# Sums of two key tiles added once more by VectorE, in halves, for all pairs but a unit's last

## The chip, the core and the metric

One core of a Trainium2 chip runs the whole program. The metric is the device time of one execution in microseconds. Its engines are TensorE (PE in the profile), VectorE (DVE), ScalarE (ACT), GpSimd (POOL) and SyncE (SP), which issues the DMAs.

## The reference

```python
x = layernorm(x + attention(x, Wq, Wkv, Wo))      # x: 2 x 2048 x 1024, 32 heads of 32, one shared k and v
x = layernorm(x + W x + b + lora(x))              # one of four ranks per row, chosen by a gate
# attention:
scores = einsum('bqhd,bkd->bhqk', q, k) * scale
bias = slopes[:, None, None] * (pos[None, None, :] - pos[None, :, None])
scores = where(causal, scores + bias, -inf)
attn = softmax(scores, axis=-1)
out = einsum('bhqk,bkd->bqhd', attn, v)
```

Only the attention is touched. What matters here is the softmax's denominator: for every query and head, the sum of the exponentials over all keys up to the query.

## The kernel before, in words

The queries of a batch row are cut into four segments of 512 (`QB`, `NSEG`), the 32 heads into eight groups of four (`GH`, `HG`). A **unit** g is one segment and one head group: 2 x 4 x 8 = 64 units, in order, each segment's eight in a row. A unit of segment s (0 to 3) has 4, 8, 12 or 16 **key tiles** of 128 keys (`ktiles`), the last four of them on the diagonal and narrower with each. A **step** k is one key tile; a **slot** is one key tile and one head, so a unit has 16, 32, 48 or 64 slots, and slot number is 4k + h.

For each slot TensorE makes the scores, keys on partitions, 512 queries wide (L895, into one of two or three PSUM banks `ps_s`, `ps_m`), and ScalarE takes the exponential into one of eight SBUF buffers `prob`, each of which holds the four heads of a key tile, 128 x 2048 float32 (L603). A step later TensorE multiplies the exponentials with the values into `ps_o` (plan item PV) and with ones into `ps_sum`, the denominators. Both go through `over_keys` (L828): four matmuls of 32 columns, one per head, which the profile records as eight. Such a set is called a group below.

To save groups on `ps_sum`, GpSimd adds the exponentials of two key tiles, a **pair** (item ADD, L540, in place in the even tile's buffer), once step 2j + 1 has its exponentials (`e_done`) and the even tile's PV is through (`pv_done`). TensorE then needs one group for two tiles (item SP, L912). All pairs are summed but a unit's last (`pairs_summed`: 0, 3, 5 and 7 per unit); the last two tiles, and every tile of the first segment, have groups of their own (SM). In the fourth segment the first two pairs of each unit are added once more by GpSimd (`QUADS = (0, 0, 0, 1)`, item ADDQ, L545), and one group covers four tiles (SQ, L915). GpSimd also splits the next unit's Wq (item WS, L514) and divides the previous unit's output by its denominators (L521). It works through its items in the order of the plan.

Beside this work on unit g, the softmax's shift for the next two units is prepared: item A is a matmul of queries against keys, 128 queries by 512 keys, for its maximum alone (L816, into one of three PSUM banks `ps_a`), which VectorE reduces (L682; L685 with the mask on the diagonal). The matmul for maximum c waits until maximum c - 3 is read (`a_done`, L815). CV reduces the maxima over chunks (L691), CT transposes them (L823, L697). Items Q and QE make the queries of unit g + 2: TensorE's projection into `ps_m` (L782 to L784), then ScalarE (L565) and VectorE (L671) split them. X, KV and VT prepare the next segment's keys and values, R turns and inverts the denominators (L707 to L714), WO loads the output matrix near the end (VectorE's part is L751, a subtraction of two SBUF tensors of 128 x 1024). After the attention follows a part that the change doesn't touch (L920 on).

`plan_unit` (L181) writes out the order of one unit's items, slot by slot; every engine walks the same list and does its part of each item, so it is the instruction order on each queue. The places are the constants in L127 to L143, one value per segment, in slots: `A_END` and `A_FROM` where the maxima of the next unit and of the one after it lie, `CHUNKS_AHEAD` how many of them are made two units ahead, `PV_AT` and `SM_AT` at which head of a step the groups on `ps_o` and `ps_sum` stand, `THIRD` from where the scores may use a third bank. Where items share a slot, the score matmul comes first, then the listed items in the order in which they were put, then PV, SM, SP, SQ.

Of the kernel before, what the change touches and what calls it, by code (L numbers as in the profile page):

```python
# [18 lines left out]
GH = P // DH  # L19
# [55 lines left out]
def pairs_summed(g):  # L75

    return ktiles(g) // 2 - 1 if full_tiles(g) else 0


def quads_summed(g):  # L80

    return QUADS[seg_of(g) % NSEG]


def adds_in(g):
    return pairs_summed(g) + quads_summed(g)


def adds_before(g):
    return sum(adds_in(x) for x in range(g))  # L90


def adds_until(g, k):

    pair = k // 2
    quad = pair // 2
    if quad < quads_summed(g):
        return adds_before(g) + 3 * quad + 1 + pair % 2
    return adds_before(g) + quads_summed(g) + pair + 1


def ring(sg):
# [21 lines left out]

CHUNKS_AHEAD = (7, 14, 18, 19)  # L127
A_END = (8, 17, 31, 41)
A_FROM = (13, 18, 31, 41)
Q_AT = ((0, 0.5), (0, 1), (1, 1.25), (0, 1.75))  # L130
QE_AT = ((3, 1), (7, 2), (9, 3), (12, 4))
CT_AT = (12, 22, 35, 42)
X_AT = ((4, 0.25), (8, 1.75), (19, 1.5), (19, 3.25))
THIRD = (6, 6, 2, 4)
QUADS = (0, 0, 0, 1)
QUAD_AT = 7
WO_AT = ((36, 6), (4, 8))
KV_AT = (10, 23, 33, 41)
VT_AT = (17, 28, 47, 49)
PV_AT = (1, 1, 2, 1)  # L140
SM_AT = (2, 1, 2, 1)
WS_AT = (5, 21, 31, 28)
RECIP_AT = ((0, 2, 3, 4, 11), (0, 2, 3, 5, 14), (0, 2, 5, 7, 18), (0, 2, 4, 5, 20))  # L143


# [35 lines left out]
def plan_unit(g):  # L181
# [6 lines left out]
    def put(slot, what, arg):  # L188
        at.setdefault(min(slots - 1, int(slot)), []).append((what, arg))
# [21 lines left out]
    if g + 2 < UNITS:  # L211
        ahead = a_chunks(g + 2)[:chunks_ahead(g + 2)]
        for i, x in enumerate(ahead):
            put(A_FROM[s] + i * (slots - A_FROM[s]) / len(ahead), "A", (g + 2, i, x))
    if g + 2 >= UNITS:
        half = DC // 2
        for i in range(half):
            put(WO_AT[g + 2 - UNITS][0] + i * WO_AT[g + 2 - UNITS][1], "WO", (g + 2 - UNITS) * half + i)
# [3 lines left out]
    for k in range(n):  # L222
        for h in range(GH):
            i = k * GH + h
            out += [x for x in at.get(i, []) if x[0] == "X"]
            out.append(("S", (k, h)))
            if g and i in recip_at:
                out.append(("R", recip_at[i]))
            out += [x for x in at.get(i, []) if x[0] != "X"]
            if k and h == PV_AT[s]:  # L230
                out.append(("PV", k - 1))
            if k > 2 * summed and h == SM_AT[s]:
                out.append(("SM", k - 1))
            if k >= 4 and k % 2 == 0 and 2 * quads <= k // 2 - 2 < summed and h == SM_AT[s]:
                out.append(("SP", k // 2 - 2))
            if k >= QUAD_AT and (k - QUAD_AT) % 4 == 0 and (k - QUAD_AT) // 4 < quads and h == SM_AT[s]:
                out.append(("SQ", (k - QUAD_AT) // 4))
        if k % 2 and k // 2 < summed:
            out.append(("ADD", k // 2))
        if k % 4 == 3 and k // 4 < quads:  # L240
            out.append(("ADDQ", k // 4))
    if summed:
        out.append(("SP", summed - 1))
    out += [("PV", n - 1), ("SM", n - 1)]
# [41 lines left out]
def attention(nc, sb, pb, sem, slopes, xb, wq_v, wkv, wo_v, w_v, att, slope_rows, ident, woh, wol, work, raw_in,  # L286
              at_sb, at_out, later):
    with ExitStack() as ctx:
# [46 lines left out]
        def counter(name):  # L335

            counters.append(sem(name))
            return counters[-1]
# [40 lines left out]
        a_done = counter("a_done")  # L379
        pv_done = counter("pv_done")  # L380
        pair_done = counter("pair_done")
        sm_done = counter("sm_done")
        VEC_C = 2 * NH + 3 + QT + SEGS + QT + 8

# [109 lines left out]
        def _(pool):  # L494
# [32 lines left out]
            def step(g, plan, count):  # L527
                steps = steps_before(g)
                for what, arg in plan:
# [4 lines left out]
                    if what == "ADD":  # L534
# [4 lines left out]
                        pool.wait_ge(pv_done, START + steps + k + 1)  # L539
                        nc.gpsimd.tensor_tensor(even[:, :, c1:], even[:, :, c1:], odd[:, :, c1:],  # L540
                                                ALU.add).then_inc(pair_done, 1)
                    if what == "ADDQ":
                        one, two = (prob[slot_of(steps + 4 * arg + i)] for i in (0, 2))
                        pool.wait_ge(pair_done, START + adds_until(g, 4 * arg + 3))
                        nc.gpsimd.tensor_tensor(one[:], one[:], two[:], ALU.add).then_inc(pair_done, 1)  # L545

            units(prologue, step, lambda count: divide(UNITS - 1))

# [65 lines left out]
        def _(dve):  # L614
# [60 lines left out]
            def maximum(count, g, i, chunk):  # L675
# [7 lines left out]
                else:  # L683
                    dve.sem_inc(went_on, 1)
                    nc.vector.tensor_tensor_reduce(ps, ps, maska[:, QB - cols:], 1.0, MASKED, ALU.add, ALU.max,  # L685
                                                   top).then_inc(a_done, 1)

            def reduce_max(g, count):
                s = seg_of(g) % NSEG
                dve.wait_ge(a_done, START + count)  # L690
                nc.vector.tensor_reduce(mx[:], mxp[:, :, 0:s + 1], AX.X, ALU.max).then_inc(c_max, 1)  # L691
# [37 lines left out]
            def step(g, plan, count):  # L729
                for what, arg in plan:  # L730
# [5 lines left out]
                        take_v(seg_of(g) + 1)  # L736
                    if what == "QE":
                        take_q(g + 2, [arg])
                    if what == "A":
                        maximum(count, *arg)  # L740
                    if what == "CV":
# [19 lines left out]
        def _(pe):  # L761
# [92 lines left out]
            def step(g, plan, count):  # L854
                steps = steps_before(g)
                for what, arg in plan:
# [51 lines left out]
                        pe.wait_ge(e_done, START + GH * (steps + arg + 1))  # L908
                        over_keys(g, ps_sum, ones[:], arg).then_inc(sm_done, 1)
                    if what == "SP":  # L910
                        pe.wait_ge(pair_done, START + adds_until(g, 2 * arg + 1))
                        over_keys(g, ps_sum, ones[:], 2 * arg).then_inc(sm_done, 2)  # L912
                    if what == "SQ":
                        pe.wait_ge(pair_done, START + adds_until(g, 4 * arg + 3) + 1)
                        over_keys(g, ps_sum, ones[:], 4 * arg).then_inc(sm_done, 4)  # L915

            units(prologue, step, lambda count: None)
# [443 lines left out]
```

## Time and profile before

| what | us |
|---|---|
| median of 3 runs | 3644.59 (3644.48 to 3645.17) |
| the profiled execution | 3642.94 |
| its span, first to last instruction | 3641.2 |
| one steady unit of segments 1, 2, 3, 4 | 20.84, 33.38, 47.24, 60.24 |

The attention takes the time up to about 2793 us, the rest the remainder. In the profile, busy time is what an engine's instructions cover; matmuls are pipelined, so that their records overlap and the distance from start to start tells what one costs. "x8" behind a name is the number of records merged into one row. An instruction's duration is given from its start, and starts behind its semaphore waits; idle time before it stands in brackets with what released it.

### The profile page before, as it was taken

What the parts mean: (1) busy time and instruction counts of PE and PEld (TensorE: products, weight loads), DVE (VectorE), ACT (ScalarE), POOL (GpSimd) and SP (SyncE); (2) the same over time, 40 slices, a digit from 0 to 9 for tenths busy, and PEclk for the clock granted to TensorE, in tenths of its full rate; (3) what the DMA queues carried; (4) which work ended last, traced back from release to release, by engine and by line L of the source; (5) the groups of instructions that cost most, each with busy time, mean ns of one, the idle gap of its engine ahead of it and who ended that gap; (6) DMA issues with size and microseconds to landing.
All of it is one profiled execution on the core that took longest, in us unless ns stands there. A gap on an engine that the chain in (4) does not pass through costs nothing. (4 is left out here: it accounts for less than half of the span.)

```text
span 3641.2 us, 56102 instructions
## 1 busy us (share of the span) xinstructions
PE 3481.5 (96%) x20833; PEld 2190.3 (60%) x20833; DVE 2290.6 (63%) x5375; ACT 1866.5 (51%) x3188; POOL 1431.2 (39%) x435
## 2 busy tenths in 40 slices
PE   5999999999999999999999999999998999999998
PEld 4555555555454554555555555454544899999997
DVE  4577777776777772677777776777762444455444
ACT  2546656665667666546656665667675101111100
POOL 1115444554657556115444554657574101011010
PEclk8999999999999999999999999999998999999999
DMA  2221110001000010221110000000012122121221
GB/s 79 55 61 30 35 48 24 25 24 42 18 19 19 19 41 19 57 62 30 36 48 24 24 24 19 19 19 18 13 58 83 47 69 65 56 69 56 65 69 41
DMA packets 158395, 148.33 MB, mean 41 GB/s; under 512 B 9396, under 2 KB 141492, under 8 KB 156056
## 3 DMA queue, kind: packets, MB, share of 16 engines
q1 hardware_dynamic: 158168, 145.34, 13.5%
q8 instruction: 139, 2.28, 0.3%
q14 instruction: 88, 0.72, 0.1%
HBM read 94.39 MB, written 33.62 MB: 35 GB/s over the span
## 5 line engine op out<-in xcount | busy, mean ns | idle before, releaser
L603 ACT ACTIVATE prob<-ps_s,alibi 128x512 f32<-128x512 f32 (+3 forms) x2119 | 1287.2, 633 | 741.6 <-PE ps_s L895 377.9
L540 POOL TENSOR_TENSOR prob<-prob 128x2048 f32<-128x2048 f32 (+1 forms) x240 | 1047.8, 4369 | 977.7 <-ACT prob L603 977.4
L682 DVE TENSOR_REDUCE mxp<-ps_a 128x1 f32<-128x512 f32 x1536 | 978.5, 682 | 296.0 <-PE ps_a L816 284.2
L816 PE MATMUL ps_a<-wol,qst 97*128 97x512 f32 (+3 forms) x2560 | 954.8, 395 | 37.0 <-DVE mxp L685 17.6
L895 PE MATMUL ps_s<-qst,kexp 97*128 97x512 f32 (+3 forms) x2119 | 862.7, 411 | 44.2 <-ACT prob L603 28.5
L895 PEld LDWEIGHTS ps_s<-qst,kexp 97*128 97x128 f32 x2119 | 399.0, 189 | 563.8 <-ACT prob L603 321.5
L685 DVE CUSTOM_DVE_ANT_0 ps_a<-ps_a,maska 128x128 f32<-128x128 f32 (+3 forms) x1024 | 492.4, 507 | 243.8 <-PE ps_a L816 233.3
L828 PE MATMUL ps_o<-prob,val 128*32 128x512 f32 (+3 forms) x5120 | 603.5, 543 | 9.9 <-ACT prob L603 6.6
L816 PEld LDWEIGHTS ps_a<-wol,qst 97*128 97x128 f32 x2560 | 486.5, 194 | 112.7 <-DVE mxp L685 31.9
L1089 POOL TENSOR_TENSOR work<-work,bias_b 128x1024 f32<-128x1024 f32 x32 | 76.9, 2402 | 745.4 <-DVE work L1228 710.9
L828 PE MATMUL ps_sum<-prob,ones 128*32 128x512 f32 (+2 forms) x3072 | 332.5, 505 | 3.7 <-POOL prob L540 3.3
L514 POOL TENSOR_TENSOR wol<-wq_raw,wol 128x1024 fp32r<-128x1024 f32 x64 | 152.5, 2383 | 449.8 <-ACT wol L558 449.8
L603 ACT ACTIVATE prob<-ps_m,alibi 128x512 f32<-128x512 f32 (+3 forms) x441 | 255.2, 579 | 116.6 <-PE ps_m L898 75.0
L1113 ACT ACTIVATE root<-var 128x1 f32<-128x1 f32 x64 | 13.0, 203 | 581.6 <-DVE var L1172 581.6
L1295 PE MATMUL ps_z<-wth,hth 128*128 128x364 f32 x768 | 255.6, 333 | 5.4 <-DVE htl L1250 5.4
L1297 PE MATMUL ps_z<-wtl,hth 128*128 128x364 f32 x768 | 252.8, 329 | 0.0
L1299 PE MATMUL ps_z<-wth,htl 128*128 128x364 f32 x768 | 252.8, 329 | 0.0
L782 PE MATMUL ps_m<-woh,wol 128*128 128x512 f32 x576 | 232.3, 403 | 3.2 <-DVE woh L646 2.8
L784 PE MATMUL ps_m<-woh,wol 128*128 128x512 f32 x576 | 230.0, 399 | 0.0
L783 PE MATMUL ps_m<-woh,wol 128*128 128x512 f32 x576 | 228.9, 397 | 0.0
L671 DVE SCALAR_TENSOR_TENSOR qst<-ps_m,qst 32x512 fp32r<-32x512 f32 x256 | 176.1, 688 | 80.0 <-ACT qst L565 73.4
L828 PEld LDWEIGHTS ps_o<-prob,val 128*32 128x32 f32 x5120 | 105.7, 108 | 188.1 <-ACT prob L603 119.8
(129 smaller groups left out, 3994.7 us busy)
## 6 DMA issues: line engine op xcount, KB each, us to landing
wq_raw<-in_L_attn_Wq SPq DMA_DIRECT2D x64, 512.0 KB, 3.5
work<-in_L_attn_hidden_states SPq DMA_DIRECT2D x8, 2048.0 KB, 8.3
qst<-qst SPq DMA_DIRECT2D x64, 256.0 KB
att_scratch<-at_sb SPq DMA_DIRECT2D x64, 256.0 KB, 2.8
at_raw<-att_scratch SPq DMA_DIRECT2D x32, 512.0 KB, 5.2
work<-in_L_attn_hidden_states SPq DMA_DIRECT2D x32, 512.0 KB, 4.1
out<-work SPq DMA_DIRECT2D x32, 512.0 KB, 3.1
work<-in_L_attn_Wo SPq DMA_DIRECT2D x8, 512.0 KB, 4.1
```

The source lines that it names most:

```text
L540: nc.gpsimd.tensor_tensor(even[:, :, c1:], even[:, :, c1:], odd[:, :, c1:], ALU.add).then_inc(pair_done, 1)
L603: nc.scalar.activation(prob[slot_of(steps + k)][:, h, c0:], ps_s[places[GH * (steps + k) + h][0]][:, c0:], ACT.Exp, bias=alibi_of(g, h, k ...
L682: nc.vector.tensor_reduce(top, ps, AX.X, ALU.max).then_inc(a_done, 1)
L685: nc.vector.tensor_tensor_reduce(ps, ps, maska[:, QB - cols:], 1.0, MASKED, ALU.add, ALU.max, top).then_inc(a_done, 1)
L782: nc.tensor.matmul(ps, wh, mh, start=start, stop=False)
L784: return nc.tensor.matmul(ps, wl, mh, start=False, stop=stop)
L816: last = nc.tensor.matmul(ps[:, 0:cols], qst[buf][0:KR, h, t * P:(t + 1) * P], kmax[0:KR, ring(sg):ring(sg) + cols], start=True, stop=True)
L828: last = nc.tensor.matmul(ps[h * DH:(h + 1) * DH, c0:], weights, prob[slot_of(steps_before(g) + k)][:, h, c0:], start=k == 0, stop=k == kt ...
L895: last = nc.tensor.matmul(bank[:, c0:], kexp[0:KR, at:at + P], qst[g % 3][0:KR, h, c0:], start=True, stop=not diagonal)
L1295: nc.tensor.matmul(ps, hth[:, c], wth[:, c, piece(p)], start=c == 0, stop=False, skip_group_check=True)
L1297: nc.tensor.matmul(ps, hth[:, c], wtl[:, c, piece(p)], start=False, stop=False, skip_group_check=True)
L1299: last = nc.tensor.matmul(ps, htl[:, c], wth[:, c, piece(p)], start=False, stop=False, skip_group_check=True)
```

## The change

The pairs that are summed are all (but a unit's last) added once more, by VectorE in place of GpSimd: one quad per unit of the second segment, two in the third, three in the fourth (`QUADS = (0, 1, 2, 3)`). The new plan item DQ stands twice per quad, each time for two of the four heads (128 x 1024 elements from each of two buffers), at slots `DQ_AT` counted from the quad's first slot, behind the other items listed at that slot. VectorE waits there for the quad's second pair add. TensorE's group on the sum (SQ) stands in step 4q + 7 and waits for both halves (`quad_done`). The pairs' and quads' counts have semaphores of their own. Thirteen lines of constants have new values, for the first segment as well.

```diff
@@ counts
-def adds_in(g):
-    return pairs_summed(g) + quads_summed(g)
-def adds_before(g):
-    return sum(adds_in(x) for x in range(g))
-def adds_until(g, k):
-    pair = k // 2
-    quad = pair // 2
-    if quad < quads_summed(g):
-        return adds_before(g) + 3 * quad + 1 + pair % 2
-    return adds_before(g) + quads_summed(g) + pair + 1
+def pairs_before(g):
+    return sum(pairs_summed(x) for x in range(g))
+def quads_before(g):
+    return sum(quads_summed(x) for x in range(g))
@@ constants
-CHUNKS_AHEAD = (7, 14, 18, 19)
-A_END = (8, 17, 31, 41)
-A_FROM = (13, 18, 31, 41)
-Q_AT = ((0, 0.5), (0, 1), (1, 1.25), (0, 1.75))
-QE_AT = ((3, 1), (7, 2), (9, 3), (12, 4))
-CT_AT = (12, 22, 35, 42)
-X_AT = ((4, 0.25), (8, 1.75), (19, 1.5), (19, 3.25))
-THIRD = (6, 6, 2, 4)
-QUADS = (0, 0, 0, 1)
+CHUNKS_AHEAD = (5, 12, 18, 18)
+A_END = (9, 17, 31, 41)
+A_FROM = (11, 18, 31, 41)
+Q_AT = ((0, 0.5), (0, 1), (1, 1.25), (1, 1.75))
+QE_AT = ((3, 1), (7, 2), (9, 4), (12, 4))
+CT_AT = (11, 24, 35, 42)
+X_AT = ((4, 0.25), (8, 1.75), (20, 2), (19, 3.25))
+THIRD = (6, 6, 6, 4)
+QUADS = (0, 1, 2, 3)
 QUAD_AT = 7
+DQ_AT = ((21, 22), (24, 26), (25, 28), (24, 26))
-KV_AT = (10, 23, 33, 41)
-VT_AT = (17, 28, 47, 49)
+KV_AT = (9, 23, 36, 41)
+VT_AT = (18, 30, 47, 49)
 PV_AT = (1, 1, 2, 1)
-SM_AT = (2, 1, 2, 1)
-WS_AT = (5, 21, 31, 28)
+SM_AT = (2, 1, 3, 2)
+WS_AT = (7, 21, 31, 28)
@@ plan_unit
+    for quad in range(quads_summed(g)):
+        for part in range(2):
+            put(4 * GH * quad + DQ_AT[s][part], "DQ", (quad, part))
-        if k % 4 == 3 and k // 4 < quads:
-            out.append(("ADDQ", k // 4))
# the SQ item of a step now stands before its SM and SP items
@@ gpsimd
-                    if what == "ADDQ":
-                        one, two = (prob[slot_of(steps + 4 * arg + i)] for i in (0, 2))
-                        pool.wait_ge(pair_done, START + adds_until(g, 4 * arg + 3))
-                        nc.gpsimd.tensor_tensor(one[:], one[:], two[:], ALU.add).then_inc(pair_done, 1)
@@ vector
+            def add_pairs(g, quad, part):
+                heads = slice(part * GH // 2, (part + 1) * GH // 2)
+                one, two = (prob[slot_of(steps_before(g) + 4 * quad + i)][:, heads] for i in (0, 2))
+                dve.wait_ge(pair_done, START + pairs_before(g) + 2 * quad + 2)
+                nc.vector.tensor_tensor(one, one, two, ALU.add).then_inc(quad_done, 1)
+                    if what == "DQ":
+                        add_pairs(g, *arg)
@@ tensor
                     if what == "SP":
-                        pe.wait_ge(pair_done, START + adds_until(g, 2 * arg + 1))
+                        pe.wait_ge(pair_done, START + pairs_before(g) + arg + 1)
                     if what == "SQ":
-                        pe.wait_ge(pair_done, START + adds_until(g, 4 * arg + 3) + 1)
+                        pe.wait_ge(quad_done, START + 2 * (quads_before(g) + arg + 1))
                         over_keys(g, ps_sum, ones[:], 4 * arg).then_inc(sm_done, 4)
```

## Rows read from the trace of the kernel before

**Rows 1.** The page: busy time of each engine over the span.
```profile
PE 3481.5 (96%) x20833; PEld 2190.3 (60%) x20833; DVE 2290.6 (63%) x5375; ACT 1866.5 (51%) x3188; POOL 1431.2 (39%) x435
```

**Rows 2.** Windows of one unit per segment: length, PE, PEld, DVE, ACT, POOL busy, clock.
```profile
130.16:151.00 20.84, 19.57 (x141) 11.65 (x145) 12.80 (x42) 11.99 (x23) 3.61 (x2) 1.00 0.21 52
347.20:380.58 33.38, 32.32 (x213) 17.95 (x209) 23.11 (x58) 22.38 (x39) 16.26 (x7) 1.00 0.13 33
670.18:717.42 47.24, 46.38 (x291) 24.43 (x291) 33.02 (x74) 32.07 (x55) 25.37 (x8) 1.00 0.09 24
1039.03:1099.27 60.24, 59.95 (x363) 30.86 (x361) 43.07 (x89) 41.86 (x70) 39.07 (x12) 1.00 0.07 19
```

**Rows 3.** Groups by line: busy us, mean ns | idle before, and what ended it.
```profile
L828 PE MATMUL ps_sum<-prob,ones 128*32 128x512 f32 (+2 forms) x3072 | 332.5, 505 | 3.7 <-POOL prob L540 3.3
...
L816 PE MATMUL ps_a<-wol,qst 97*128 97x512 f32 (+3 forms) x2560 | 954.8, 395 | 37.0 <-DVE mxp L685 17.6
...
L540 POOL TENSOR_TENSOR prob<-prob 128x2048 f32<-128x2048 f32 x192 | 880.6, 4590 | 925.7 <-ACT prob L603 925.7
...
L545 POOL TENSOR_TENSOR prob<-prob 128x2048 f32<-128x2048 f32 x16 | 74.2, 4639 | 1.3
```

**Rows 4.** Timeline of TensorE, two steps of a fourth segment's unit: start, duration.
```profile
1171.49 1.07 PE L828 MATMUL ps_o<-prob,val 128*32 128x512 f32 x8
1172.38 1.04 PE L828 MATMUL ps_sum<-prob,ones 128*32 128x512 f32 x8
1173.35 0.50 PE L895 MATMUL ps_s<-qst,kexp 97*128 97x512 f32 x1
...
1174.96 0.39 PE L895 MATMUL ps_s<-qst,kexp 97*128 97x512 f32 x1
1175.19 0.40 PE L816 MATMUL ps_a<-wol,qst 97*128 97x512 f32 x1
1175.52 1.06 PE L828 MATMUL ps_o<-prob,val 128*32 128x512 f32 x8
1176.52 0.50 PE L895 MATMUL ps_m<-qst,kexp 97*128 97x512 f32 x1
...
1178.61 0.64 PE L828 MATMUL ps_o<-prob,val 128*32 128x512 f32 x4
```

**Rows 5.** Timeline of VectorE (L751) and GpSimd in the last two units.
```profile
2722.22 4.18 DVE L751 TENSOR_TENSOR wol<-work,woh 128x1024 fp32r<-128x1024 f32 x1 [3.73 <-ACT woh L594]
2727.61 1.23 DVE L751 TENSOR_TENSOR wol<-work,woh 128x1024 fp32r<-128x1024 f32 x1 [1.22 <-ACT woh L594]
...
2756.93 1.98 DVE L751 TENSOR_TENSOR wol<-work,woh 128x1024 fp32r<-128x1024 f32 x1 [4.77 <-ACT woh L594]
...
2720.74 4.58 POOL L540 TENSOR_TENSOR prob<-prob 128x2048 f32<-128x2048 f32 x1 [3.38 <-ACT prob L603]
...
2756.55 1.28 POOL L521 TENSOR_TENSOR at_sb<-work 128x512 f32<-128x512 f32 x1
```

**Rows 6.** Timeline, fourth segment, around slot 24: VectorE's part of Q, then TensorE.
```profile
1158.79 0.70 DVE L671 SCALAR_TENSOR_TENSOR qst<-ps_m,qst 32x512 fp32r<-32x512 f32 x1 [0.19 <-ACT qst L565]
...
1157.84 0.40 PE L816 MATMUL ps_a<-wol,qst 97*128 97x512 f32 x1
1158.16 1.06 PE L828 MATMUL ps_o<-prob,val 128*32 128x512 f32 x8
...
1160.27 0.44 PE L816 MATMUL ps_a<-wol,qst 97*128 97x384 f32 x1
```

**Rows 7.** Timeline of GpSimd and VectorE, third segment, around slots 25 and 41.
```profile
720.61 4.59 POOL L540 TENSOR_TENSOR prob<-prob 128x2048 f32<-128x2048 f32 x1 [1.90 <-ACT prob L603]
...
721.00 0.73 DVE L685 CUSTOM_DVE_ANT_0 ps_a<-ps_a,maska 128x512 f32<-128x512 f32 x1
...
682.97 8.04 POOL L540 TENSOR_TENSOR prob<-prob 128x2048 f32<-128x2048 f32 x2
...
687.17 2.48 DVE L682 TENSOR_REDUCE mxp<-ps_a 128x1 f32<-128x512 f32 x4 [0.83 <-PE ps_a L816]
```

More of the change, by code:

```diff
@@ L231, in plan_unit @@
                 out.append(("PV", k - 1))
+            if k >= QUAD_AT and (k - QUAD_AT) % 4 == 0 and (k - QUAD_AT) // 4 < quads and h == SM_AT[s]:
+                out.append(("SQ", (k - QUAD_AT) // 4))
             if k > 2 * summed and h == SM_AT[s]:
@@ L235, in plan_unit @@
                 out.append(("SP", k // 2 - 2))
-            if k >= QUAD_AT and (k - QUAD_AT) % 4 == 0 and (k - QUAD_AT) // 4 < quads and h == SM_AT[s]:
-                out.append(("SQ", (k - QUAD_AT) // 4))
         if k % 2 and k // 2 < summed:
             out.append(("ADD", k // 2))
-        if k % 4 == 3 and k // 4 < quads:
-            out.append(("ADDQ", k // 4))
     if summed:
@@ L381, in attention @@
         pair_done = counter("pair_done")
+        quad_done = counter("quad_done")
         sm_done = counter("sm_done")
```

## The prediction

> **What bounds the kernel now.** I read the engine totals first: TensorE is busy for 3481.5 us of the 3641.2 us span, VectorE for 2290.6, GpSimd for 1431.2 [rows 1]. The next view is one steady unit of the second, third and fourth query segment [rows 2]. A unit of eight key tiles takes 33.4 us, one of twelve 47.2, one of sixteen 60.2. TensorE is busy for all but 0.3 to 1.1 us of each, always at full granted clock; VectorE is idle for 10.3, 14.2 and 17.2 us. So attention is bound by TensorE, and VectorE seems to have room. Busy time flatters TensorE, because its matmuls overlap in the records; starts tell more.
>
> Rows 4 are such starts, in a unit of sixteen key tiles. A step with a group for the denominators (eight records on ps_sum) runs from 1171.49 to 1175.52, 4.03 us; the next one without it from 1175.52 to 1178.61, 3.09 us. A removed group is worth about the difference, so what is removed lies on the path.
>
> **What the change removes.** Groups per unit, from the plan: five, seven and eight before (second, third, fourth segment), four, five and six after. That is 1 + 2 + 2 = 5 fewer over three units, times 16 units of each kind (eight head groups, two batch rows) = 80 groups, all 512 wide. The records on ps_sum should fall from 3072 [rows 3] by 640 to 2432. Price of a group that stands right behind one on ps_o: the pair takes 1171.49 to 1173.35 = 1.86 us, the ps_o group alone 1175.52 to 1176.52 = 1.00 us, so 0.86; 0.88 by the start of ps_sum behind ps_o [rows 4]. I take 0.87: 80 x 0.87 = 70 us less.
>
> **What moves.** SM_AT goes from 2 to 3 and from 1 to 2 in the third and fourth segment, while PV_AT stays at 2 and 1: the groups for sums inside a unit no longer stand behind one on ps_o, but a slot later. A group that stands by itself needs 1.00 us to the next score matmul and starts 0.33 us behind its predecessor (1175.19 to 1175.52), where the usual step from one to the next is 0.23; against 0.87 that is 0.13 + 0.10 = 0.23 more [rows 4]. Such places: two in a unit of the third segment, three in one of the fourth, 80 in all: 80 x 0.23 = 18 us. Gross gain: 70 - 18 = 52 us.
>
> GpSimd loses 16 adds of 4.64 us, 74 us [rows 3]. GpSimd is busy for 39 of 60 us at most [rows 2], so this alone gives no time; but the add behind it in its queue starts sooner. The other constants move maxima by a few slots, also in the first segment, where no sum changes. No instruction and no DMA is added by them. I put them at nothing; they could give or take some 0.2 us a unit (an estimate from the 0.3 to 1.1 us in which TensorE is not busy [rows 2]), 64 units, so 13 us either way. What hides a late transposed maximum (CT_AT 22 to 24 and so on) are the five or more slots left in its unit.
>
> **What it adds.** Six quads over three units, 96 in all, each with two VectorE adds of 128x1024: 192 instructions. The trace has the same form, VectorE adding or subtracting two SBUF tensors of 128x1024: 1.23 us where nothing disturbs it (the one at 2727.61) [rows 5]. That makes 236 us, or 7.4 us in a unit of the fourth segment, which has 17.2 idle. Were that all, the adds would be hidden.
>
> **Why I don't leave it there.** Two other L751 rows took 4.18 and 1.98 us [rows 5]. Each ended 1.08 us after a GpSimd instruction on SBUF that was running when it started: 2726.40 after 2725.32, 2758.91 after 2757.83. So an add of VectorE waits for the whole rest of the GpSimd instruction and then does its work. The new adds have the same operands (two from SBUF), and GpSimd's pair adds, 4.59 us each [rows 3], are the instructions they meet. The Trainium skill's page "SBUF — State Buffer", section "Who interferes with whom", says it as a rule: a VectorE instruction with two SBUF inputs contends with a GpSimd instruction that reads SBUF, and the later one blocks; without that rule the sum would end at the gross gain, with it the waits below are owed, and the trace agrees (4.18 against 1.23 us).
>
> Do they meet? The planner puts the first half at slots 24 (second and fourth segment) and 25 (third) of a quad's sixteen. At slot 24 the exponentials of the quad's sixth key tile end, and for them GpSimd starts its third pair add. Three places can be read:
> - Fourth segment, first quad. VectorE comes to slot 24's end at 1159.49, behind its part of Q. GpSimd, rid of its quad add, which held it back here, starts the third pair add with the exponentials, at the latest at 1158.16, when the ps_o group on the same exponentials starts; it runs to 1162.7. VectorE waits 3.2 us and ends at 1163.8. Maxima have three PSUM banks: the matmuls from 1157.84 on fill them, the fourth, due at 1160.27, waits until the oldest is read (0.69 us), 1164.5. TensorE stands for 4.2 us [rows 6].
> - Third segment, first quad: VectorE is there at 721.7, GpSimd adds from 720.61 to 725.20; VectorE ends at 726.3. The fourth matmul is due at about 723.3 (0.4 us apart behind the ps_o group) and gets a bank at 726.6: 3.3 us [rows 7].
> - Third segment, second quad: VectorE at 688.5 in the middle of its four maxima, GpSimd in the second of its two adds until 691.0; VectorE ends at 692.1, the fourth matmul waits from about 691.9 to 692.8: 0.9 us [rows 7].
> The mean is 2.8 us. I take 2.6, as VectorE may be first where both arrive together. Part comes back: a step without a sum group takes 3.09 us for some 2.7 us of starts, and after a stall ScalarE has caught up, so two steps give back 0.4 each: 2.6 - 0.8 = 1.8 us a quad. The second half, two or three slots later, I put at nothing: it falls into VectorE's catching up, with TensorE slow already; without that cover it costs its 1.2 us. Queued behind the stalled TensorE are score matmuls, so ScalarE and then GpSimd run dry, and the sum group of the quad, three or four slots after the second half, waits too.
>
> **Sum.** 96 x 1.8 = 173, less 52: +121 us. The profiled execution took 3642.9 us, 1.65 below the median of the runs, 3644.6. 3644.6 + 121 = 3766 us. Ends of the unknown: 0.8 us a quad gives 77 - 52 = +25, 3670; 2.9 us (the mean with nothing given back) gives 278 - 52 = +226, 3871. As a check, the fourth segment's VectorE would hold 43.1 + 7.4 + 3 x 3.2 = 60.1 us [rows 2], all of the unit, before any wait for TensorE, which it cannot avoid while Q is computed.
>
> **Rivals.**
> - Faster: the waits stay small or are covered. VectorE gets between GpSimd's adds (once the unit is shorter, its places drift against the exponentials), or the banks and VectorE's idle time take up what is left. For it speak the idle 10 to 17 us a unit, against it the three places read above. It gives the gross gain, 3644.6 - 52 = 3593 us; with 0.4 us left per quad 3631. The point that decides is 0.54 us a quad (52 / 96). Chance 0.27.
> - Slower without blocking: VectorE's order alone. A half put between maxima delays them by 1.23 us, the two by 2.5, against banks worth about 0.8 to 2.3 us; the sum group waits for the second half. One us a quad gives 96 - 52 = +44, 3689 us. Chance 0.12.
> - A draw at about 0.5 us a quad: within 7 us of before. Chance 0.05.
> - The change doesn't remove what it says: the count 2432 would fail. The plan gives it directly, so I leave this under 0.01.
> My forecast has 0.56, with a range of its own of 3670 to 3870.
>
> **Numbers.** 0.2% (7 us) is about what a measurement of this kernel can tell from no change. Slower: 0.56 + 0.12 = 0.68. Same 0.05. Faster 0.27. The range reaches from the gross gain, 3592, to 3845: it leaves out about a tenth below and less than a tenth above.
>
> **What would show it.** Right: L545 gone from GpSimd, 192 VectorE adds with a mean well over 1.23 us and a longest of 4 to 5.8; their long ones end 1.1 us after a GpSimd add; waits of TensorE for the maxima's VectorE lines, now 37 us before L816 [rows 3], go to 100 us and more; units of the fourth segment longer by most. Wrong: the adds at 1.2 to 1.3 us, units at about 32, 46 and 59 us. If the adds are long and the time still falls, the slack was mis-sized, not the blocking. The first segment's units, 20.8 us, should stay.

## The result, and the profile after

| | before | after |
|---|---|---|
| median of 4 runs each, same chip, us | 3644.88 | 4102.77 (4084.17 to 4117.80) |
| ratio, 95% interval | | 1.125 (1.119 to 1.131) |
| profiled execution / its span | 3642.94 / 3641.2 | 4091.74 / 4090.0 |
| mean granted clock of TensorE | 0.988 | 0.931 |
| typical unit, segments 2, 3, 4 | 33.4, 47.2, 60.2 [rows 2] | 38.0, 56.4, 75 to 79 |

The change costs 458 us, 12.5%. Slower was forecast, but by 121 us, and the range ended at 3845. The page of the changed kernel, its engine totals and four of its groups (busy us, mean ns | idle before, and what ended it):

```profile
PE 3674.8 (90%) x20193; PEld 2227.2 (54%) x20193; DVE 2753.0 (67%) x5567; ACT 1880.4 (46%) x3188; POOL 1373.5 (34%) x419
...
L534 POOL TENSOR_TENSOR prob<-prob 128x2048 f32<-128x2048 f32 (+1 forms) x240 | 1059.4, 4414 | 1390.1 <-ACT prob L593 1390.1
L815 PE MATMUL ps_a<-wol,qst 97*128 97x512 f32 (+3 forms) x2560 | 1006.3, 413 | 200.1 <-DVE mxp L672 124.3
L683 DVE TENSOR_TENSOR prob<-prob 128x1024 f32<-128x1024 f32 x192 | 489.7, 2553 | 35.6 <-POOL prob L534 35.1
L827 PE MATMUL ps_sum<-prob,ones 128*32 128x512 f32 (+3 forms) x2432 | 317.2, 625 | 44.1 <-DVE prob L683 43.6
```

TensorE has 640 records less than before [rows 1] and yet 193 us more of busy time: the same matmuls have become longer. The records on ps_sum are 2432, as planned, at 625 ns where they took 505 [rows 3]. The adds take 2.55 us in the mean, twice their undisturbed 1.23 [rows 5], so about 250 us of the 489.7 are waits inside the instruction. Of the 192 adds 118 begin while a GpSimd instruction runs: all of these end 1.08 or 1.09 us after it, and take 3.39 us in the mean; the other 74 take 1.21. TensorE's idle time before the maxima went from 37 us [rows 3] to 200, and all of its idle time from 159.7 to 415.2 us (span less busy time). The windows of one unit of each segment (columns as in [rows 2]):

```profile
136.22:157.34 21.12, 19.61 (x139) 11.58 (x139) 12.77 (x42) 11.77 (x23) 3.59 (x3) 1.00 0.19 51
359.28:397.26 37.98, 33.97 (x206) 18.71 (x206) 27.56 (x61) 22.18 (x39) 17.16 (x6) 0.96 0.12 29
783.96:840.40 56.44, 51.33 (x277) 24.73 (x273) 42.63 (x78) 32.69 (x54) 25.35 (x8) 0.91 0.07 20
1233.54:1312.84 79.30, 68.78 (x349) 33.61 (x353) 59.37 (x96) 42.70 (x71) 34.75 (x11) 0.85 0.05 14
```

In the second, third and fourth segment TensorE now stands for 4.0, 5.1 and 10.5 us of a unit, and the column behind GpSimd's, its granted clock, is no longer 1.00. The loss lies in both. One quad shows how they hang together: the first of the unit at 1233.54, in the timeline of GpSimd, VectorE and TensorE (start, duration).

```profile
1236.31 4.56 POOL L534 TENSOR_TENSOR prob<-prob 128x2048 f32<-128x2048 f32 x1 [1.49 <-ACT prob L593]
...
1238.63 3.33 DVE L683 TENSOR_TENSOR prob<-prob 128x1024 f32<-128x1024 f32 x1
...
1238.96 0.40 PE L894 MATMUL ps_m<-qst,kexp 97*128 97x512 f32 x1
...
1242.73 0.44 PE L815 MATMUL ps_a<-wol,qst 97*128 97x384 f32 x1 [3.38 <-DVE mxp L672]
```

The half starts at 1238.63, GpSimd's pair add ends at 1240.87, the half at 1241.96, 1.09 us later (the two L751 rows of [rows 5] had 1.08). The maxima in VectorE's queue behind it are late, their banks stay full, and TensorE stands for 3.38 us. What follows is in windows of 2 us (the column behind GpSimd's is the clock):

```profile
1239.54:1241.54 2.00, 0.00 (x0) 0.00 (x0) 2.00 (x1) 1.94 (x3) 1.34 (x1) 1.00 0.61 131
...
1243.54:1245.54 2.00, 2.00 (x10) 0.45 (x9) 2.00 (x2) 0.59 (x1) 0.65 (x1) 0.67 0.00 0
1245.54:1247.54 2.00, 1.92 (x10) 0.49 (x9) 1.55 (x8) 0.69 (x1) 0.00 (x0) 0.50 0.00 0
1247.54:1249.54 2.00, 2.00 (x8) 1.35 (x5) 0.34 (x1) 0.71 (x2) 0.00 (x0) 0.50 0.00 0
1249.54:1251.54 2.00, 2.00 (x12) 0.88 (x11) 1.67 (x8) 1.31 (x2) 1.94 (x1) 0.50 0.03 8
1251.54:1253.54 2.00, 2.00 (x11) 0.94 (x4) 0.00 (x0) 0.20 (x1) 2.00 (x1) 0.50 0.00 0
1253.54:1255.54 2.00, 2.00 (x10) 1.29 (x13) 1.57 (x5) 1.99 (x4) 0.61 (x1) 0.77 0.00 0
1255.54:1257.54 2.00, 2.00 (x15) 1.13 (x8) 1.17 (x7) 1.31 (x3) 0.00 (x0) 1.00 0.00 0
```

TensorE is busy nearly throughout after the stall, but from 1243.5 to 1255.5 the granted clock is 0.67, 0.50 and 0.77, so at 1.2 GHz for most of it. Against 1.00 that is (0.33 + 4 x 0.50 + 0.23) x 2 = 5.1 us, more than the stall itself. This is the dearest case: over the 95 stalls of more than 1.5 us in the attention, 2.87 us long in the mean, the clock lost in the same way from the stall's end to the next stall (or for 14 us) is 2.3 us in the mean, 0 to 5.1, and 4 of them lose nothing. Over the program (1 - 0.931) x 4090 = 282 us against (1 - 0.988) x 3641 = 44 before: 238 us more, or 2.5 per quad, an upper end, since some of it lies where TensorE stands anyway and some comes with the moved constants (below). At half clock the ps_o group to the next score takes 1.87 us, in this unit at full clock 0.99.

The Trainium skill, page "TensorE: Matmul & The Clock Gate", section "HAM oscillation — how this bites in real kernels", describes this: a wait between bursts of matmuls that lets the clock fall makes each next burst start at the lower clock, every time again. There the wait is for a DMA, here for VectorE; the trace agrees with the mechanism, if not for every stall (91 of the 95 above).

### The profile page after: what moved, and what is told of

Its sections match the earlier page's. It is cut to its first block and busy times, and to the rows that moved or that the text cites. A ratio compares the mean times of both kernels' runs of the same rounds, so it can differ in the third digit from the quotient of the medians.

```text
span 4090.0 us, 54999 instructions
## 1 busy us (share of the span) xinstructions
PE 3674.8 (90%) x20193; PEld 2227.2 (54%) x20193; DVE 2753.0 (67%) x5567; ACT 1880.4 (46%) x3188; POOL 1373.5 (34%) x419
## 5 line engine op out<-in xcount | busy, mean ns | idle before, releaser
L593 ACT ACTIVATE prob<-ps_s,alibi 128x512 f32<-128x512 f32 (+3 forms) x2161 | 1313.9, 631 | 995.3 <-PE ps_s L897 535.6
L534 POOL TENSOR_TENSOR prob<-prob 128x2048 f32<-128x2048 f32 (+1 forms) x240 | 1059.4, 4414 | 1390.1 <-ACT prob L593 1390.1
L815 PE MATMUL ps_a<-wol,qst 97*128 97x512 f32 (+3 forms) x2560 | 1006.3, 413 | 200.1 <-DVE mxp L672 124.3
L894 PE MATMUL ps_s<-qst,kexp 97*128 97x512 f32 (+3 forms) x2161 | 913.5, 428 | 31.1 <-DMA qst<-shift_t 14.5
L894 PEld LDWEIGHTS ps_s<-qst,kexp 97*128 97x128 f32 x2161 | 423.9, 196 | 637.2 <-ACT prob L593 382.0
L815 PEld LDWEIGHTS ps_a<-wol,qst 97*128 97x128 f32 x2560 | 508.5, 202 | 319.0 <-DVE mxp L672 161.6
L827 PE MATMUL ps_o<-prob,val 128*32 128x512 f32 (+3 forms) x5120 | 646.5, 579 | 9.6 <-ACT prob L593 6.2
L683 DVE TENSOR_TENSOR prob<-prob 128x1024 f32<-128x1024 f32 x192 | 489.7, 2553 | 35.6 <-POOL prob L534 35.1
L827 PE MATMUL ps_sum<-prob,ones 128*32 128x512 f32 (+3 forms) x2432 | 317.2, 625 | 44.1 <-DVE prob L683 43.6
L593 ACT ACTIVATE prob<-ps_m,alibi 128x512 f32<-128x512 f32 (+3 forms) x399 | 229.0, 574 | 235.7 <-PE ps_m L894 167.5
L508 POOL TENSOR_TENSOR wol<-wq_raw,wol 128x1024 fp32r<-128x1024 f32 x64 | 155.4, 2429 | 539.4 <-ACT wol L548 539.4
```

Source lines behind the costliest of these rows:

```text
L593: nc.scalar.activation(prob[slot_of(steps + k)][:, h, c0:], ps_s[places[GH * (steps + k) + h][0]][:, c0:], ACT.Exp, bias=alibi_of(g, h, k ...
L683: nc.vector.tensor_tensor(one, one, two, ALU.add).then_inc(quad_done, 1)
L815: last = nc.tensor.matmul(ps[:, 0:cols], qst[buf][0:KR, h, t * P:(t + 1) * P], kmax[0:KR, ring(sg):ring(sg) + cols], start=True, stop=True)
L827: last = nc.tensor.matmul(ps[h * DH:(h + 1) * DH, c0:], weights, prob[slot_of(steps_before(g) + k)][:, h, c0:], start=k == 0, stop=k == kt ...
L894: last = nc.tensor.matmul(bank[:, c0:], kexp[0:KR, at:at + P], qst[g % 3][0:KR, h, c0:], start=True, stop=not diagonal)
```

## The experiments

Two theories to start with. **A**: an add of VectorE waits out GpSimd's running instruction, and that wait sets the time. **B**: the halves' length and place in VectorE's queue, or the moved constants, do. Each time below is set against the kernel before of its own call (3645 to 3650 us).

### GpSimd writes, and reads nothing

```diff
-  nc.gpsimd.tensor_tensor(even[:, :, c1:], even[:, :, c1:], odd[:, :, c1:], ALU.add)
+  nc.gpsimd.memset(even[:, :, c1:], 1.0)
```

The sums of pairs are left out; VectorE and TensorE do all of theirs.

> The changed kernel, but GpSimd fills the even tile of a pair with ones in place of adding the two (the denominators are not computed; values, maxima and all waits stay), so it no longer reads SBUF there. Theory A (VectorE's adds wait for GpSimd's pair adds, TensorE then stalls and its granted clock falls): the 192 VectorE adds take 1.2 to 1.3 us but for a few that meet L508 or L515, the clock is 0.98 or more, the time is near the gross gain, 3590 to 3620 us. Rival B (VectorE's order alone, no blocking): the adds already took their time elsewhere and the time stays above 3690 us.

3695.0 us, ratio 1.013 (1.010 to 1.016), +45. Its group and a unit of the fourth segment:

```profile
L682 DVE TENSOR_TENSOR prob<-prob 128x1024 f32<-128x1024 f32 x192 | 238.6, 1245 | 23.5 <-POOL prob L534 23.1
```
```profile
1170.76:1232.57 61.81, 59.91 (x349) 30.03 (x345) 48.92 (x96) 42.13 (x71) 16.05 (x10) 1.00 0.07 18
```

The adds are at their 1.24 us, none over 1.60, the clock of this unit is full, and 413 of the 458 us are gone: A. But 3590 to 3620 us were expected and 3695 came, by the time alone a case for B: what is left above the gross gain is B's part, and is taken up below. A memset is also shorter than the add (1.72 us in the mean against 4.41), but length is not what frees VectorE here: 41 adds begin while a memset runs and take 1.22 us all the same, while the 14 that begin beside the split of Wq (L508), which reads SBUF, end 1.08 us after it. The Trainium skill's page "SBUF — State Buffer", section "Who interferes with whom", says that GpSimd instructions that only write don't contend with such an add; nothing here speaks against it.

With the constants of before, the same two kernels:

> The changed kernel (quads 0, 1, 2, 3 and both halves at the places of DQ_AT) with every other place constant as before. Theory A (blocking, then the clock): as slow as the changed kernel or nearly, 3900 to 4150 us, clock under 0.95, adds of 2.3 us or more on average. Rival C: under 3800 us.

> As the last one, with GpSimd filling the even tile with ones in place of adding (the denominators are not computed). The same kernel with the new places took 3695 us. If the remainder above the gross gain (100 us) is VectorE's order (its 1.2 us halves against three PSUM banks, and the transposed maximum behind them), it stays: 3660 to 3730 us. If it is the new places, it goes: 3580 to 3620 us.

4099.1 us, 1.124 (1.120 to 1.127), and 3688.9, 1.011 (1.008 to 1.014): +451 and +41. The gap is 410 again, so the moved constants are not the cause; both times lie in their expected ranges.

### One quad a unit, VectorE in GpSimd's place

The kernel before in constants and groups (`QUADS = (0, 0, 0, 1)`), but its 16 quads added in VectorE's two halves.

> The kernel before with one thing changed: the one quad of a fourth segment's unit (16 in all) is added by VectorE in two halves at slots 24 and 26 in place of by GpSimd; all places are those of before. No group on ps_sum is saved. Theory A: the first half waits 3 us for GpSimd in each of the 16 units, TensorE stalls for 3 to 4 us and then runs at a lower clock for some us: 4 to 8 us a unit, 3710 to 3770 us, with a clock below 0.985 in the fourth segment. Rival B: VectorE's 2.5 us more per unit are hidden or cost at most their length, 3645 to 3685 us. Rival C (the new places of the other items cause most of the loss): 3645 to 3660 us here.

3736.0 us, 1.024 (1.021 to 1.027), +86: 5.4 us for each of 16 quads, where no group was won. Adds 3.02 us in the mean. The stall and the windows behind it:

```profile
1181.52 0.50 PE L815 MATMUL ps_a<-wol,qst 97*128 97x384 f32 x1 [3.56 <-DVE mxp L672]
```
```profile
1182.40:1184.40 2.00, 2.00 (x10) 0.38 (x12) 2.00 (x4) 0.69 (x1) 0.55 (x1) 0.50 0.00 0
1184.40:1186.40 2.00, 2.00 (x16) 0.75 (x9) 1.20 (x5) 0.06 (x1) 0.00 (x0) 0.81 0.00 0
```

### No quads at all, in the new places

`QUADS = (0, 0, 0, 0)` in the changed kernel.

> The changed kernel with QUADS all 0: no quad anywhere, so VectorE adds nothing and meets nothing; only the new places are left. Against the kernel before it has 16 groups on ps_sum more (14 us) and 160 groups that stand by themselves (37 us at 0.23). If the places are neutral, as the prediction put them: 3685 to 3705 us, clock as before. Rival C, the places cost by themselves: over 3720 us.

3716.7 us, 1.019 (1.016 to 1.022), +68, with no adds on VectorE. It has 16 groups more than before, and 192 groups (five in a third segment's unit, seven in a fourth's; the expectation counts 160, without the last single tiles) stand a slot behind the values instead of right behind them. By the prediction's prices that is 16 x 0.87 + 192 x 0.23 = 58, which leaves 10 for the other constants; the last of the three kernels without adds, below, finds 16. The time lies between the two expectations (up to 3705, from 3720) and decides for neither.

### GpSimd's add in pieces

```diff
+  for i in range(4):                    # 2 in the other
+      cut = slice(i, i + 1)
+      nc.gpsimd.tensor_tensor(even[:, cut, c1:], ..., odd[:, cut, c1:], ALU.add)
```

> The changed kernel, but GpSimd adds each pair in four instructions, one per head, of 128x512. What VectorE can meet is then 1.2 us long in place of 4.6. Theory A: VectorE's adds take 1.2 to 2.5 us, mean under 1.9; no stall of TensorE long enough for its clock to fall, clock 0.98 or more; time 3590 to 3650 us. Rival B (VectorE's order): near the changed kernel, over 3900 us.

> The changed kernel, but GpSimd adds each pair in two instructions of 128x1024, 2.4 us each. If the loss is the wait itself, in proportion to it (A1), half of the 510 us between the gross gain and the measured time goes: about 3850 us. If most of it is the clock that falls only after a long stall (A2), the stalls of up to 2 us no longer lower it: clock 0.98 or more and 3620 to 3720 us.

Quarters: 3814.3 us, 1.045 (1.042 to 1.048), +164, adds 1.65 us in the mean. Halves: 3828.6, 1.049 (1.039 to 1.059), +178, adds 1.90. Quarters were to give 3590 to 3650: missed. Halves came out near the 3850 that the waits in proportion would give; that a shorter wait would leave the clock alone is refuted, it was 0.967 to 0.974 where 0.98 was expected. The waits beyond 1.245 us sum to 251 us after, 125 with halves, 78 with quarters; the time above the write-only kernel is 413, 133, 119. So it falls with the waits, if not in proportion: with half of the waits a third of the time is left. Halves and quarters can't be told apart (the halves' time is uncertain by some 37 us either way), and GpSimd is itself busy for 1302 us on quarters and 1185 on halves where the whole adds took 1059. Quarters also failed to bound a wait by one piece, in the last unit:

```profile
2926.22 13.33 POOL L536 TENSOR_TENSOR prob<-prob 128x512 f32<-128x512 f32 x10
...
2934.68 7.09 DVE L685 TENSOR_TENSOR prob<-prob 128x1024 f32<-128x1024 f32 x2 [7.34 <-POOL prob L536]
...
L685 DVE TENSOR_TENSOR prob<-prob x192: 1201/1608/5952, 300.3 to 2951.4; 128x1024 f32<-128x1024 f32 x192
```

(The last row has the shortest, middle and longest add in ns.) Ten pieces run back to back until 2939.55, the last of them 1.27 us each. The first of the two adds starts at 2934.68, is the longest, 5.95 us, and ends at 2940.63, 1.08 after the last piece: three pieces that began behind it (2935.83, 2937.07, 2938.29) went first. That is rare: of the 176 adds that begin beside a GpSimd instruction four let later pieces pass, and with halves two of 163; the rest end 1.08 to 1.16 us after the one that they met.

### Places between GpSimd's adds

`DQ_AT = ((21, 22), (22, 22), (23, 23), (23, 24))`, old constants otherwise: slots where GpSimd seemed idle in the trace of before.

> The old places, with the halves where GpSimd is mostly idle, between the end of a quad's second pair add and the start of the next: slots 22 and 22, 23 and 23, 23 and 24 for the second, third and fourth segment. Theory A: the adds take 1.2 to 1.3 us in the second and third segment, where GpSimd is idle at that slot; in the fourth segment's second and third quad GpSimd works without a pause and blocks them or VectorE waits for the pair. 3650 to 3800 us, clock 0.96 or more. Rival B (order alone): no faster than the one with DQ_AT as changed.

4303.3 us, 1.179 (1.176 to 1.183), +655: worse than the change, and far outside the 3650 to 3800 expected.

```profile
1232.32 4.54 POOL L534 TENSOR_TENSOR prob<-prob 128x2048 f32<-128x2048 f32 x1 [1.41 <-ACT prob L593]
...
1232.71 5.22 DVE L683 TENSOR_TENSOR prob<-prob 128x1024 f32<-128x1024 f32 x1
...
L683 DVE TENSOR_TENSOR prob<-prob 128x1024 f32<-128x1024 f32 x192 | 590.9, 3100 | 49.5 <-POOL prob L534 49.1
```

VectorE comes to its slot later than TensorE does, and so 0.39 us after GpSimd began instead of before it: it waits for nearly all of the add. As many adds meet a GpSimd instruction as in the change (112 against 118), but these take 4.45 us in the mean against 3.39.

### The halves' own length

Write-only as above, and the sums narrowed to 32 of 512 columns (the rest is left out). Then the same with GpSimd's real add, and with the second half alone narrowed.

```diff
+  one, two = one[:, :, 0:32], two[:, :, 0:32]
   dve.wait_ge(pair_done, ...)
```

> The run that took 3695 us (GpSimd only writes), with VectorE's adds cut to 32 of 512 columns (0.2 us each; the denominators are not computed). If the 100 us above the gross gain are the length of VectorE's halves in its queue, they go: 3590 to 3625 us. If they are the new places or the waits for the pairs, the time stays over 3670 us. It also checks the gross gain of 52 us itself.

> The changed kernel with VectorE's adds cut to 32 of 512 columns, GpSimd's adds as they are (the denominators are not computed). What is left is the wait for GpSimd's instruction, without the 1.1 us of work behind it. Theory A: the adds still take 1 to 4.6 us each, 1.2 us on average or more; the time lies between, 3850 to 4020 us. Rival B (the length of the halves): under 3700 us.

> The changed kernel with the second half of each quad cut to 32 of 512 columns (the denominators are not computed); the first half is whole. It lies between 3935 us (both cut) and 4103 us (none). If the second half costs nothing, as the prediction put it: 4090 us or more. If it costs as much as the first: near 4020 us. If it is the dearer one, because it comes while VectorE catches up with full banks: under 3990 us.

3638.4 us, 0.998 (0.996 to 0.999), -10; 3935.4, 1.079 (1.069 to 1.089), +287; 4055.6, 1.112 (1.109 to 1.115), +408. With adds of 0.245 us and no blocking the change is worth 10 us (3638.4 us where 3590 to 3625 were expected); length alone costs 45 + 10 = 55. Of TensorE's idle time before the maxima it makes 24 us (75.5 where it is 51.4 with the narrow halves). In the second of these kernels the adds take 1.548 us, 1.303 of it waits, 250 us in all, the same as in the change; blocking without length costs 297. Full length on top costs 458 - 287 = 171, of it 50 the second half and 121 the first (the latter uncertain by the second kernel's interval, some 37 us either way). So the two causes don't simply add: 55 us of length alone, 171 behind the blocking (the table below counts it there).

### The clock

Three groups of four matmuls with zero weights, added onto ps_o behind the score of a slot near the stall (one slot a quad; they change no value): first on the one-quad kernel, at slot 27, then on the change, at slots 28; 28, 44; 27, 41, 60 of the second, third and fourth segment. (The expectations say twelve to a group; it is twelve in all, which the profile records as 24.)

```diff
+  for _ in range(3):
+      for head in range(GH):
+          nc.tensor.matmul(ps_o[head * DH:(head + 1) * DH], maska[:, 0:DH], maska[:],
+                           start=False, stop=False)
```

> The kernel with one quad a unit (3736 us), plus three groups of twelve matmuls with zero weights on ps_o, 2.7 us at full clock, just before the place where TensorE stands 3.6 us in each of the 16 units. They add zeros, so the output stays. If the falling clock costs what the records show (about 2 us a unit behind the stall), keeping TensorE at work takes it away: 3695 to 3712 us although 43 us of matmuls are added, and the clock is back over 0.985. If the clock only follows and costs nothing, the time is 3736 us or more.

> The changed kernel plus the same three groups at each of its six stalls (96 places, 250 us of matmuls at full clock). If the clock is the larger part of what the prediction missed, 100 to 250 us go, 3850 to 4000 us, and the mean clock is over 0.96. If the waits are the loss by themselves: 4100 us or more.

3699.1 us, 1.014 (1.011 to 1.017), +51, and 3946.9, 1.082 (1.079 to 1.085), +298. A filler, the maximum after it, and the unit in the one-quad kernel:

```profile
1044.94 2.78 PE L902 MATMUL ps_o<-maska 128*32 128x512 f32 x24
...
1048.94 0.44 PE L815 MATMUL ps_a<-wol,qst 97*128 97x384 f32 x1 [0.67 <-DVE mxp L672]
...
1167.60:1231.48 63.88, 62.93 (x389) 31.59 (x385) 47.67 (x92) 41.90 (x71) 34.65 (x11) 1.00 0.07 18
```

and a third and a fourth segment's unit of the filled change, which were 56.4 at 0.91 and 79.3 at 0.85:

```profile
760.83:812.79 51.96, 51.71 (x325) 24.92 (x321) 42.70 (x78) 32.76 (x54) 25.37 (x8) 1.00 0.08 21
1256.13:1326.75 70.62, 68.49 (x421) 32.12 (x425) 57.66 (x96) 42.44 (x71) 34.61 (x11) 1.00 0.06 16
```

Work was added, 16 x 2.78 = 44 us and 96 x 2.78 = 267, and the time fell, by 35 and 160. The matmuls lie in what was TensorE's stall (3.56 us became 0.67; in the filled change the idle time before the maxima is 56 us in place of 200), and the clock stays at 1.00 (0.984 over the whole filled change). VectorE's waits are hardly less in the filled change, 2.51 us an add where they were 2.55, so of its 160 us nearly all are taken to be the clock's; in the one-quad kernel they are less too, 2.55 for 3.02, and some 15 of the 35 us may be theirs. That makes about 150 of the 458 us the clock behind the stalls, as a lower end, since the fillers are partly in the way themselves.

### The gain, without the adds

Quads as planned, VectorE's adds left out, so that the denominators lack half of each quad: with old constants; with `SM_AT` as changed; with all constants as changed.

```diff
-  if what == "DQ":
-      add_pairs(g, *arg)
...
-  pe.wait_ge(quad_done, START + 2 * (quads_before(g) + arg + 1))
+  pe.wait_ge(pair_done, START + pairs_before(g) + 2 * arg + 2)
```

> The kernel before without 80 groups on ps_sum and without the 16 quad adds of GpSimd: the plan has the quads 0, 1, 2, 3, TensorE sums only the first pair of each, nothing is added in their place (the denominators are not computed), all places are the old ones. By the prediction's 0.87 us a group: 3575 to 3590 us. If TensorE then waits for ScalarE's exponentials instead, it is about half: 3600 to 3625 us.

> As the last one, with SM_AT as changed (2, 1, 3, 2). By the prediction's 0.23 us for each of 80 groups that stand by themselves: 18 us more than the last one. If it lets ScalarE catch up between the groups, nothing or less.

> As e14, with all places as changed. The prediction put the other places at nothing, plus or minus 13 us: within 13 us of e15. If the new places are part of what is missing: 15 to 30 us slower than e15. The run with narrow adds (3638 us) is this one plus VectorE's waits for the pairs; if those cost nothing, this one is also near 3635 us.

3603.5 us, 0.988 (0.984 to 0.992), -44; 3622.8, 0.993 (0.989 to 0.996), -25; 3638.8, 0.997 (0.995 to 0.999), -9. The first two are uncertain by some 15 us either way, the third by 6, so the steps between them, 19 and 16, are known to some 20 and 14. Undisturbed units are sharper. `SM_AT` makes a third segment's 46.6 us long in place of 46.3 and a fourth's 59.4 in place of 58.5, which over 16 units each is 19; the other constants change the four segments' units by +0.3, +0.1, -0.3 and +0.2, about 5 us, and the rest of their 16 is not placed. The mean granted clock goes with it: 0.988, 0.982 and 0.981 in the three profiled executions, 24 us more clock lost in the third than in the first, over half of it in the first segment. The third kernel, which has GpSimd's real adds, equals the write-only kernel with narrow halves (-10): GpSimd's longer instruction, the waits for pairs and those for VectorE's queue cost nothing by themselves. Units of the first of these:

```profile
379.61:412.78 33.17, 31.44 (x205) 17.69 (x201) 23.07 (x58) 22.36 (x39) 16.25 (x6) 1.00 0.13 33
713.99:760.24 46.25, 44.87 (x275) 23.96 (x274) 33.08 (x73) 32.17 (x55) 25.37 (x9) 1.00 0.09 24
1143.57:1202.18 58.61, 58.33 (x349) 30.34 (x345) 43.00 (x90) 41.87 (x71) 34.60 (x10) 1.00 0.07 19
```

Against [rows 2] a unit gains 0.2, 1.0 and 1.6 us, where 0.87, 1.74 and 1.74 were forecast. In the second segment the removed group leaves 1.7 us of idle TensorE (it had 1.1); what it then waits for wasn't followed.

### More quads on GpSimd instead

`QUADS = (0, 0, 1, 1)` and `(0, 0, 1, 2)` in the kernel before.

> The kernel before with QUADS = (0, 0, 1, 1): one quad also in each unit of the third segment, added by GpSimd whole, all places as before. 16 groups fewer, at the measured 0.55 us 9 us; GpSimd has some 22 us idle in such a unit. If the add is through before slot 31, 3635 to 3642 us; if the sum group or the next pair adds come late, 3645 us or more.

> As the last one, with a second quad in each unit of the fourth segment, QUADS = (0, 0, 1, 2). GpSimd's adds stand back to back there until slot 41, so this quad's add would end about when its sum group is due (slot 46): 9 us more gained if in time, 3626 to 3634 us; if late, TensorE waits up to 2 us a unit and it is slower than the last one.

3658.3 us, 1.003 (1.002 to 1.004), +11, and 3701.7, 1.015 (1.013 to 1.017), +55. So a quad on GpSimd costs more than its group is worth; -9 was forecast for the first. There no sum group comes late (TensorE's idle time before ps_sum is 3.7 us as before), but a third segment's unit takes 48.4 us where it took 47.2, and what the add delays was not followed. In the latter kernel TensorE waits 28.6 us before ps_sum for GpSimd's quad add, and a unit of the fourth segment takes 64.8 us at clock 0.95:

```profile
1169.14:1233.93 64.79, 62.56 (x355) 31.46 (x353) 43.19 (x89) 42.03 (x70) 43.46 (x12) 0.95 0.06 17
```

No version with all of the work in it came out below the kernel before.

## Why the prediction was right and wrong

| part | forecast | measured | from |
|---|---|---|---|
| 80 groups removed | -70 | -44 | adds left out, old constants |
| `SM_AT` | +18 | +19 | the next of the three |
| other constants | 0 (13 either way) | +16 | the last of the three |
| length of the halves | 0, hidden | +55 | full against narrow, write-only |
| blocking, with what follows | +173 | +413 | change against write-only |
| sum | +121 | +459 (seen: 458) | |

The rows run from kernel to kernel in one chain, so that their sum must come out near the 458; it is no check of the parts. The forecast's 173 has the first half's own length in it, so the last two rows are best compared together. The second and third rows are uncertain by 20 and 14 us.

**Right.** The sign. The mechanism: the halves end 1.07 to 1.09 us after the GpSimd instruction that they meet (the unit's second quad: 1263.57 after 1262.50), the mean is far over 1.23, and without GpSimd's reading add 413 us are gone. The count 2432. The size of the stall: 2.8 us was read from the trace of before and 2.6 taken; six stalls in the changed kernel, three in the fourth segment's unit, two in the third's and one in the second's:

```profile
1242.73 0.44 PE L815 MATMUL ps_a<-wol,qst 97*128 97x384 f32 x1 [3.38 <-DVE mxp L672]
1263.76 0.38 PE L822 MATMUL ps_a<-ident,mx 128*16 128x128 f32 x1 [4.22 <-DVE mx L688]
1282.92 0.80 PE L815 MATMUL ps_a<-wol,qst 97*128 97x512 f32 x1 [2.57 <-DVE mxp L672]
792.07 0.50 PE L815 MATMUL ps_a<-wol,qst 97*128 97x512 f32 x1 [2.68 <-DVE mxp L675]
809.98 0.51 PE L815 MATMUL ps_a<-wol,qst 97*128 97x512 f32 x1 [2.17 <-DVE mxp L672]
414.82 1.08 PE L827 MATMUL ps_sum<-prob,ones 128*32 128x512 f32 x4 [2.22 <-DVE prob L683]
```

have a mean of 2.87 us, as the 95 have, and TensorE's idle time rose by 255.5 us, 2.66 a quad. In part this is luck: the three places were read as 4.2, 3.3 and 0.9 us and show 3.38, 2.68 and 2.17, so that the errors cancel in the mean. Two of them are not before a maximum but before the transposed maximum (L822) and before the quad's sum, which waits for the second half: places that the prediction had named at most in passing.

**Wrong.** The step that failed is "Part comes back: ... 2.6 - 0.8 = 1.8 us a quad". Per quad the change cost (413 + 55) / 96 = 4.9 us, so on balance nothing came back. After the stall TensorE was to run its queue tighter than before; instead it ran at 1.2 GHz, and the stretch at that clock cost 2.3 us behind a stall in the mean and 5.1 at most. The prediction saw "always at full granted clock" in the rows of before and priced everything behind the stalls at it, a term put at nothing without a reason. The fillers show it: with matmuls in the stalls the clock stays up, and 160 us come back by more work. The upper end, "nothing given back", 2.9 us a quad, had the same gap: the true one was the stall plus what follows it.

Second, the halves' length. "Were that all, the adds would be hidden" rested on VectorE's 17.2 idle us a unit. They cost 55 us without any blocking (0.57 per quad) and 171 under it. The idle time is not where the halves stand; they are put between maxima, and each late maximum holds a bank (24 of the 55 us are seen as TensorE's waits for maxima; where the rest lies was not followed). The main case had the first half's length only where it follows a wait, and nothing for the 1.21 us of each add that meets nothing. The prediction had this as a rival (1.0 us a quad), but the two causes don't exclude one another. Of the second half it said "at nothing ... without that cover it costs its 1.2 us"; it costs 50 / 96 = 0.52.

Third, the price of a removed group: 0.87 from starts in one place of the fourth segment, 44 / 80 = 0.55 in truth. The fourth segment nearly gave it (1.6 of 1.74), the second hardly any. A hint stood in [rows 2]: the second segment's TensorE had already 1.1 us idle in 33.4, the most of the three. That this is why the group is worth little there was not tested.

Of the rivals, "faster" came true only where both causes were taken out, and by 10 us (the write-only kernel with narrow halves); "slower without blocking" gave 3695 against its 3689. The first segment's units "should stay": 21.12 against 20.84, which is the new constants, since with the old ones the changed kernel has 20.8 again.

## What to carry to other kernels

A stall of a matmul engine that is always busy must be priced with what follows it: here 2.9 us of stall became 4.9 per quad, mostly because the granted clock fell to half behind it (the rest is the halves' length). Before an elementwise add of two SBUF operands is given to VectorE, look which GpSimd instructions that read SBUF run at that moment: here each such add ended 1.08 us after the one that it met, however long that was. To move the add to where GpSimd was idle in the old trace didn't help, since the places drift. And idle time per unit says nothing of a place: ask how many banks lie between the delayed instruction and the engine that fills them. (Three here; no run varied their number.)

## What the runs showed that was not expected

- TensorE at 1.2 GHz for some 10 us behind a stall of 3.4 us, though it was busy for nearly all of that time (windows above), and 2 to 4 us of it behind one of 3.56 us in the one-quad kernel. Even stalls of the same 3.38 us at the same place of other units lose 1.7 us of clock in some and 5.1 in others; why, is open.
- Matmuls of zero weights in the stall keep the clock at 1.00: 267 us of them made the kernel 160 us faster. It is still 298 us slower than before.
- A VectorE add that meets GpSimd instructions back to back isn't sure to be next: 5.95 us beside pieces of 1.27, in two of 176 adds. The Trainium skill's page "SBUF — State Buffer", section "Who interferes with whom", speaks of a block for the whole of an instruction; here it lasted for several, and the measurement decides.
- Blocking and length make each other worse: 55 us of length alone, 171 with blocking.
